# Experts' first matrices split into two float32r parts for the product with the stacked features, and bulk transfers moved in the SyncE queue

## The chip, the cores and the metric

One Trainium2 chip; the program runs on one of its cores. The metric is the device time in microseconds (us) of one execution, and the kernel before and the changed kernel are each run several times. Engines are named as in the profile: PE (TensorE matmuls), PEld (its weight loads), DVE (VectorE), ACT (ScalarE), POOL (GpSimd), SP (SyncE, which only issues transfers). An engine name with q behind it is that engine's instruction queue.

## The reference

The input is `x`, 8 sequences of 512 tokens of 512 numbers. Two layers are applied, each with a condition stage and a feed-forward stage.

```python
# layer 0, condition: a low-rank map chosen by the sequence's language, plus an embedding
t = einsum('bsd,brd->bsr', x, lora_A[lang]); x = einsum('bsr,bdr->bsd', t, lora_B[lang]) + embed[lang]
# layer 0, feed-forward: mixture of 8 experts, 2 for each token, capacity 512 tokens for each expert
weights = softmax(top2(x @ expert_embeddings.T)); index, vals = first 512 tokens of each expert
inter = relu(einsum('ech,eih->eci', tokens, first_linear))      # 512 -> 1024
out = einsum('eci,ehi->ech', inter, second_linear) * vals       # 1024 -> 512, added back by index
# layer 1, condition: additive attention pooling with a mask
# layer 1, feed-forward: two linear layers (512 -> 2048 -> 512), activations in int8,
# weights w1, w2 rounded to -1, 0, 1 with scale 1/mean(|w|)
```

Because the tokens that enter the experts are themselves a product of 100 stacked features (rank rows and language rows) with a matrix of 512 columns, the kernel multiplies that matrix with each expert's first matrix beforehand, and the tokens' 100 features with the result. Float32 accuracy is wanted throughout layer 0.

## The kernel before

The program has three blocks, one behind the other; a barrier stands between them.

**First block (0 to 74 us).** `x_t` is loaded in eight parts, multiplied with the projection, the tokens are routed to experts, and slots are found. The first matrices of experts 0 to 2 (2 MB each, `w_in_sb`, a ring of `AHEAD` = 3) are loaded and multiplied with `lora_b_sb` (`g_product`, L176 to L180): for each half `n` of the 1024 columns, four quarters `k` of the 512 rows, one float32 matmul of 100 x 512 each, accumulated in one PSUM bank.

**Second block (74 to 350 us), the experts.** For each expert `e` (0 to 7) there are eight steps `k` (`KI` = 8), each for 128 of the 1024 inner columns:

- PE: `inner_block` (L907 to L913) makes 128 x 512 inner values in a PSUM bank from `g_0`, `g_1` and the gathered features `rows_0`, `rows_1` with two float32r matmuls; `out_block` (L914 to L927) of the step before makes the outputs with 12 float32r matmuls; `expand` (L931 to L939) makes quarters of the product `lora_b_sb` x first matrix for the expert two further on, at steps 1, 2, 3 (first half) and 5, 6, 7 (second half) of experts 1 to 5 by the table `G_AT`: 8 products for each expert, 40 in all. At step 3 `turn` transposes the features of the next expert.
- ACT: `w_h` (L802, the rounded part of the second matrix), `inner_h` (L806), then by step `take_y`, `high_g`, `take_rows`, and the preparation of layer 1's weights: `sum_abs` (L777, 16 instructions for the mean of absolute values) and `quantise` (L789 and L793, 32 pairs).
- DVE: `w_l` (L868, what rounding left over), `inner_l` (L871), then by step `take_y` (L859), `low_g` (L850, L852), `weights`, `take_rows`. In expert 3 it sums the absolute values at step 0 (L887), PE multiplies that sum with ones at step 1 (L950) ahead of its `out_block`, and DVE makes scales of it at step 2.
- POOL: for each expert it gathers features for the expert two further on (`gather`, L185, four indirect transfers), its slots' choices (L719, four), and adds the outputs of the expert to DRAM (L739, four). The first of these additions waits until all eight parts of `x` have been copied to DRAM (`x1_init`).
- SP issues in the order written in its part (L679 to L713): copies of `x` to `x_after_experts` (1 MB each, `copy_x`), second matrices `w_raw` (1 MB halves, each waits for `w_l_cp`, that is, for DVE to have finished with the buffer), first matrices `w_in_sb` (2 MB), and layer 1's weights `raw` (1 MB groups, two buffers).

```python
def out_block(e, k):
    pe.wait_ge(in_l, KI * e + k + 1)
    pe.wait_ge(w_l_cp, KI * e + k + 1)
...
act.wait_ge(in_mm, i + 1)
if i >= 2:
    act.wait_ge(k_mm, i - 1)
act.activation(inner_h[:, k % 2, :], ps[:, 4 + k % 2, :], ACT.Relu).then_inc(in_h, 1)
```

**Third block (350 to 771 us)** is layer 1. The change doesn't touch its code.

A split into float32r parts, as the kernel uses it for the second matrices: the high part is the value rounded to float32r by a copy, the low part is value minus high part; three products (low x high, high x low, high x high) stand for one float32 product.

## Time and profile before

| | us |
|---|---|
| median of 3 runs | 775.08 |
| lowest and highest run | 775.01 and 776.08 |
| the profiled execution | 772.75 |
| its span (first to last instruction) | 770.8 |
| PE busy | 680.4 (88% of the span) |
| DVE busy | 500.3 (65%) |
| ACT busy | 485.1 (63%) |
| POOL busy | 375.7 (49%) |

The span is what the rows of the trace are measured in, from its start. The profiled execution is 1.95 us longer than its span and 2.33 us shorter than the median of the runs. PE's granted clock is 1.00 where it is at 2.4 GHz, and about half of that where it is at 1.2 GHz. In a timeline row of PE, the starts of consecutive matmuls tell what one costs; its duration is longer, since matmuls overlap. Two matmul instructions of line L179 are one float32 product.

### The profile page before, as it was taken

The numbers are of one execution on the slowest core, as the hardware profiler recorded it, in microseconds if no ns is written. First come the engines' busy times: TensorE is split into PE (matmuls) and PEld (weight loads), VectorE is DVE, ScalarE is ACT, GpSimd is POOL, SyncE is SP. The second block draws the span as 40 slices with busy tenths as digits, with TensorE's granted clock in tenths as the row PEclk, the third lists the DMA queues.
The fourth block names the chain that finished last, engine by engine and source line by source line (L and its number), as shares of the span: only waits on it lengthen the run. The fifth ranks groups of instructions, "written<-read, shape, count | busy, mean of one in ns | idle before, by whom it ended". The sixth has DMA issues, their size and how long they took to land.

```text
span 770.8 us, 9706 instructions
## 1 busy us (share of the span) xinstructions
PE 680.4 (88%) x3152; PEld 416.5 (54%) x3184; DVE 500.3 (65%) x897; ACT 485.1 (63%) x724; POOL 375.7 (49%) x386
## 2 busy tenths in 40 slices
PE   6898689998999999964778889999898998898996
PEld 3333577676777777752455554555455554454442
DVE  3287344544444555524255889888898888999893
ACT  1245236664367778841355878697786977878772
POOL 0202723554342611333575675857758566644463
PEclk9999989999999999985989999999999999999999
DMA  6997949998483937727112021031211110112211
GB/s 214 301 405 284 351 160 369 307 328 295 99 225 146 233 132 162 164 30 239 43 55 83 1 96 55 28 110 51 86 56 42 42 55 29 55 56 69 68 56 68
DMA packets 41699, 108.79 MB, mean 141 GB/s; under 512 B 5393, under 2 KB 6177, under 8 KB 38449
## 3 DMA queue, kind: packets, MB, share of 16 engines
q1 hardware_dynamic: 33712, 94.64, 34.7%
q0 software_dynamic: 7424, 13.06, 9.4%
q10 hardware_dynamic: 512, 0.47, 0.2%
q8 instruction: 25, 0.41, 0.2%
q14 instruction: 26, 0.20, 0.1%
HBM read 88.42 MB, written 28.13 MB: 151 GB/s over the span
## 4 chain that ended last, share of the span: by engine, by line
PE 16%; issue 12%; DVE 11%; POOL 9%; ACT 3%; DVEq 1%; POOLq 0%; ACTq 0%
PE ps L1253 5%; PE ps L1279 5%; POOL ht L1225 3%; POOL xb L1231 2%; DVE h L1686 2%; DVE h_mx L1691 2%; DVE run_max L1652 1%; DVE pool_mx L1608 1%; DVE run_max L1653 1%; PE ps L1303 1%; PE ps L1310 1%; POOL rms L1208 1%; DVEq L1645 1%; POOL qt L1176 1%; PE ps L1312 1%
## 5 line engine op out<-in xcount | busy, mean ns | idle before, releaser
L1253 PE MATMUL ps<-ff_q,qt 128*128 128x512 bf16 x486 | 120.8, 390 | 11.4 <-DVE h L1686 5.1
L1279 PE MATMUL ps<-ff_q,ht 128*128 128x512 bf16 x506 | 121.3, 383 | 4.5 <-DVE res L1699 4.3
L739 POOL DMA_INDIRECT x_after_experts<-y,row_of_slot x32 | 51.2, 1599 | 138.1 <-DVE y L859 109.3
L922 PE MATMUL ps<-w_h,inner_l 128*128 128x512 f32 x256 | 103.7, 405 | 10.0 <-issue 6.6
L924 PE MATMUL ps<-w_h,inner_h 128*128 128x512 f32 x256 | 101.5, 396 | 0.0
L923 PE MATMUL ps<-w_l,inner_h 128*128 128x512 f32 x256 | 101.4, 396 | 0.0
L1686 DVE SCALAR_TENSOR_TENSOR h<-ps,scale,bias 128x1024 f32<-128x1024 f32 x64 | 81.9, 1280 | 24.2 <-PE ps L1253 24.1
L871 DVE SCALAR_TENSOR_TENSOR inner_l<-ps,inner_h 128x512 fp32r<-128x512 f32 x64 | 44.2, 690 | 71.6 <-ACT inner_h L806 53.8
L806 ACT ACTIVATE inner_h<-ps 128x512 fp32r<-128x512 f32 x64 | 38.0, 593 | 82.2 <-PE ps L912 58.5
L1253 PEld LDWEIGHTS ps<-ff_q,qt 128*128 128x128 bf16 x512 | 48.2, 100 | 68.9 <-DVE h L1686 10.2
L1480 ACT ACTIVATE h<-h 128x1024 f32<-128x1024 f32 x64 | 66.7, 1052 | 24.9 <-DVE h L1686 24.7
L1279 PEld LDWEIGHTS ps<-ff_q,ht 128*128 128x128 bf16 x512 | 49.3, 99 | 59.8 <-DVE res L1699 4.6
L1691 DVE TENSOR_REDUCE h_mx<-h 128x1 f32<-128x1024 f32 x64 | 77.4, 1210 | 2.0 <-ACT h L1480 2.0
L868 DVE TENSOR_TENSOR w_l<-w_raw,w_h 128x512 fp32r<-128x512 f32 x64 | 44.2, 690 | 51.3 <-ACT w_h L802 49.2
L1486 ACT ACTIVATE h<-h,to_q 128x2048 int8<-128x2048 f32 x32 | 63.9, 1998 | 13.2 <-DVE to_q L1712 13.2
L1225 POOL TENSOR_SCALAR ht<-hp 128x2048 bf16<-128x2048 int8 x32 | 60.8, 1899 | 5.9 <-DVE hp L1675 5.2
L1554 ACT ACTIVATE h_junk<-h 128x2048 int8<-128x2048 f32 x32 | 61.1, 1911 | 1.0
L922 PEld LDWEIGHTS ps<-w_h,inner_l 128*128 128x128 f32 x256 | 49.0, 192 | 22.4 <-issue 7.0
L179 PE MATMUL ps<-w_in_sb,lora_b_sb 128*100 128x512 f32 x128 | 60.7, 595 | 0.0
L1204 POOL TENSOR_SCALAR mean_sq<-h_sq 128x1 f32<-128x1 f32 x32 | 6.1, 190 | 110.9 <-ACT h_junk L1554 110.8
L924 PEld LDWEIGHTS ps<-w_h,inner_h 128*128 128x128 f32 x256 | 49.0, 191 | 11.5
L923 PEld LDWEIGHTS ps<-w_l,inner_h 128*128 128x128 f32 x256 | 49.2, 192 | 10.4
(251 smaller groups left out, 1330.2 us busy)
## 6 DMA issues: line engine op xcount, KB each, us to landing
w_in_sb<-in_w_in_t SPq DMA_DIRECT2D x8, 2048.0 KB
w_raw<-in_w_out_t SPq DMA_DIRECT2D x16, 1024.0 KB
raw<-in_ff_t SPq DMA_DIRECT2D x16, 1024.0 KB
x_after_experts<-in_x SPq DMA_DIRECT2D x8, 1024.0 KB
x_sum<-x_after_experts SPq DMA_DIRECT2D x8, 1024.0 KB, 4.9
x<-x_after_experts SPq DMA_DIRECT2D x32, 256.0 KB, 2.7
out<-res SPq DMA_DIRECT2D x32, 256.0 KB, 2.3
x_sum<-in_x_t SPq DMA_DIRECT2D x6, 1024.0 KB, 6.6
```

Of the source, the lines that this page charges most:

```text
L179: return pe.matmul(ps[0:STACK_1, bank, :], lora_b_sb[:, k, :], w_in_sb[:, e % AHEAD, k, n * 512:(n + 1) * 512], start=k == 0, stop=k == KD ...
L922: pe.matmul(ps[:, s, :], inner_l[:, k % 2, c], w_h[:, k % RING, :], start=k == 0, stop=False)
L923: pe.matmul(ps[:, s, :], inner_h[:, k % 2, c], w_l[:, k % RING, :], start=False, stop=False)
L924: m = pe.matmul(ps[:, s, :], inner_h[:, k % 2, c], w_h[:, k % RING, :], start=False, stop=k == KI - 1)
L1225: pool.tensor_scalar(ht[:, t % 2, :, :, :], pairs, 1.0, 0.0, ALU.mult, ALU.add).then_inc(ht_ready, 1)
L1253: m = pe.matmul(ps[:, ff_bank(t, half) + n, :], qt[:, t // TPB % 2, t % TPB, k, :], ff1_q[:, k, f * 512:(f + 1) * 512], start=k == 0, stop ...
L1279: mm = pe.matmul(ps[:, out_bank(t), :], ht[:, t % 2, k // 2, k % 2, :], ff2_q[:, k, :], start=k == 0, stop=k == KF - 1)
L1480: act.activation(part, part, ACT.Gelu).then_inc(gelu, 1)
L1486: act.activation(h8[:, t % 2, :], h[:, t % 2, :], ACT.Copy, scale=to_q2[:, t % 2:t % 2 + 1]).then_inc(h8_ready, 1)
L1554: act.activation(h_junk[:], h[:, t0 % 2, :], ACT.Square, accum_out=h_sq[:, t0 % 2:t0 % 2 + 1]).then_inc(h_squared, 1)
L1686: ve.scalar_tensor_tensor(h[:, t % 2, cols], ps[:, bank:bank + 2, :].rearrange("p a c -> p (a c)"), scale1[:, t:t + 1], bias1[:, cols], AL ...
L1691: ve.tensor_reduce(h_mx[:, t % 2, half:half + 1], h[:, t % 2, half * HALF:(half + 1) * HALF], AX.X, ALU.max, apply_absolute_value=True).th ...
```

## The change

1. In the second block each 2 MB first matrix of experts 3 to 7 is no longer multiplied as float32. POOL makes the high part of one quarter (128 x 512) at a time (`split_high`), DVE the low part (`split_low`), each into a ring of `G_RING` = 4; `lora_b_sb` is split once, in expert 0 at step 2 (`u_h` by ACT, `u_l` by DVE). PE makes three float32r products in place of one float32 product. POOL and DVE wait for `part_mm` before a place of the ring is written again.
2. `split_high` stands in POOL's queue: the second half of expert `e + 2` behind the gather of iteration `e`, the first half of expert `e + 3` ahead of its additions.
3. `w_in_sb` becomes a list of separate tensors, three in the first block and two in the second; SP's load of one waits for `win_l_cp`.
4. `raw` and `rounded` use the memory of `x_sum`. SP's queue is rearranged: two copies of `x` and the first two groups of `raw` come later.
5. `sum_abs` runs from expert 1 step 7 to expert 3 step 6 (before: experts 1 and 2), the sum and scale in expert 4 at steps 0 and 1 (before: expert 3, steps 0 and 2), and `quantise` from expert 4 step 2, with two pairs at steps 0 and 1 of expert 7.

```diff
+            w_in_sb = w_in_sb + [sb(a, "w_in_sb2", [P, KD, INNER])]
...
-            QUANT_AT = 4 * KI
+            ABS_AT = 2 * KI - 1
+            QUANT_AT = 4 * KI + 2
+            G_RING = 4
...
+            u_h, u_l = (sb(a, f"u_{i}", [P, KD, STACK_1], F32R) for i in "hl")
+            win_h, win_l = (sb(a, f"win_{i}", [P, G_RING, 512], F32R) for i in "hl")
...
-            raw = sb(a, "raw", [P, 2, GK, D])
+            raw = [x_sum[1], sb(a, "raw", [P, GK, D])]
...
-            rounded = sb(a, "rounded", [P, 2, D])
+            rounded = x_sum[0][:, 0:2, :]
...
+            def quant_steps(e, k):
+                n = e * KI + k - QUANT_AT + max(0, min(k, 2)) * (e == EXPERTS - 1)
+                return range(max(n, 0), n + 1 + (e == EXPERTS - 1 and k < 2))
...
+            part_of = lambda e, n, k: (e - G_FIRST) * 2 * KD + n * KD + k
...
                     sp.wait_ge(rows_in[0], DMA * SB)
-                    for b in (2, 3, 4):
-                        copy_x(sp, b)
+                    copy_x(sp, 2)
...
                             if e + 1 < EXPERTS:
                                 sp.wait_ge(w_l_cp, e * KI + (i + 1) * KI // 2)
                                 sp.dma_start(w_raw[:, i, :, :], w_out_v[e + 1, i]).then_inc(w_raw_in[i], DMA)
                             if e == 0:
-                                load_raw(i)
-                                for b in ((5,), (6, 7))[i]:
+                                for b in ((3, 4), (5, 6, 7))[i]:
                                     copy_x(sp, b)
-                            if e in (1, 2):
-                                load_raw(4 * e - 1 + 2 * i)
+                            if e == 1:
+                                load_raw(i)
...
+                    def split_high(e, n):
+                        for k in range(KD) if G_FIRST <= e < EXPERTS else ():
+                            u = part_of(e, n, k)
+                            if n == 0 and k == 0:
+                                pool.wait_ge(w_in_in[w_in_at(e)], DMA * ((e - G_FIRST) // 2 + 2))
+                            if u >= G_RING:
+                                pool.wait_ge(part_mm, u - G_RING + 1)
+                            pool.tensor_scalar(win_h[:, u % G_RING, :], w_in_sb[w_in_at(e)][:, k, n * 512:(n + 1) * 512],
+                                               1.0, 0.0, ALU.mult, ALU.add).then_inc(win_h_cp, 1)
...
                             gather(pool, e + 2)
+                            split_high(e + 2, 1)
                             pool.wait_ge(w_slot_ready, e + 1)
                             gather_choices(e + 2)
+                        split_high(e + 3, 0)
...
+                    def split_low(e, n, k):
+                        u = part_of(e, n, k)
+                        ve.wait_ge(win_h_cp, u + 1)
+                        if u >= G_RING:
+                            ve.wait_ge(part_mm, u - G_RING + 1)
+                        ve.tensor_tensor(win_l[:, u % G_RING, :], w_in_sb[w_in_at(e)][:, k, n * 512:(n + 1) * 512],
+                                         win_h[:, u % G_RING, :].bitcast(F32), ALU.subtract).then_inc(win_l_cp, 1)
...
+                            if 1 <= e <= EXPERTS - AHEAD:
+                                for n, part in G_AT.get(k + 1, ()):
+                                    split_low(e + 2, n, part)
...
-                            m = g_product(pe, e, n, part, G_BANK)
-                            if part == KD - 1:
-                                m.then_inc(g_mm, 1)
+                            pe.wait_ge(win_l_cp, u + 1)
+                            bank = ps[0:STACK_1, G_BANK, :]
+                            pe.matmul(bank, u_l[:, part, :], win_h[:, u % G_RING, :], start=part == 0, stop=False)
+                            pe.matmul(bank, u_h[:, part, :], win_l[:, u % G_RING, :], start=False, stop=False)
+                            pe.matmul(bank, u_h[:, part, :], win_h[:, u % G_RING, :], start=False, stop=part == KD - 1).then_inc(part_mm, 1)
```

POOL's queue in experts 0 and 1, before (L185 is a gather of features, L719 of choices, L739 the addition of an expert's outputs):

```order
L185 DMA rows<-token_features,row_of_slot 128x100 x4
L719 DMA choices<-token_choices,row_of_slot 128x4 x4
L739 DMA x_after_experts<-y,row_of_slot 4608x512 x4
L185 DMA rows<-token_features,row_of_slot 128x100 x4
L719 DMA choices<-token_choices,row_of_slot 128x4 x4
```

and in the change (line numbers are those of the changed kernel: L736 choices, L769 addition, L748 the high part):

```order
L185 DMA rows<-token_features,row_of_slot 128x100 x4
L736 DMA choices<-token_choices,row_of_slot 128x4 x4
L748 ISA
L748 TENSOR_SCALAR win_h<-w_in_sb 128x512 x4
L769 DMA x_after_experts<-y,row_of_slot 4608x512 x4
L185 DMA rows<-token_features,row_of_slot 128x100 x4
L748 TENSOR_SCALAR win_h<-w_in_sb 128x512 x4
```

The second set of four high parts, which is the second half of expert 3's matrix, stands behind the first additions and a gather.

SP's queue at the start of the second block, before:

```order
L154 DMA x_after_experts<-in_x 128x4x512 [waits rows_in0]
L154 DMA x_after_experts<-in_x 128x4x512 x2
L691 DMA w_in_sb<-in_w_in_t 128x4096
L698 DMA w_raw<-in_w_out_t 128x4x512 [waits w_l_cp]
L686 DMA raw<-in_ff_t 128x2048
L154 DMA x_after_experts<-in_x 128x4x512
L698 DMA w_raw<-in_w_out_t 128x4x512 [waits w_l_cp]
L686 DMA raw<-in_ff_t 128x2048
L154 DMA x_after_experts<-in_x 128x4x512 x2
```

and in the change:

```order
L154 DMA x_after_experts<-in_x 128x4x512 [waits rows_in0]
L707 DMA w_in_sb<-in_w_in_t 128x4096
L715 DMA w_raw<-in_w_out_t 128x4x512 [waits w_l_cp]
L154 DMA x_after_experts<-in_x 128x4x512 x2
L715 DMA w_raw<-in_w_out_t 128x4x512 [waits w_l_cp]
L154 DMA x_after_experts<-in_x 128x4x512 x3
```

Two of the three copies ahead of the first matrix now stand behind the first `w_raw`, and both groups of `raw` are gone from this piece.

DVE's queue in the change, expert 4, steps 0 and 1 (L893 `take_y`, L884 and L886 `low_g`, L900 the low part of a quarter, L934 the sum of absolute values, L910 `w_l`, L913 `inner_l`):

```order
L893 TENSOR_SCALAR y<-ps,w_slot 128x512 x2
L884 TENSOR_TENSOR g<-ps,g 64x512
L886 TENSOR_TENSOR g<-ps,g 4x512
L900 TENSOR_TENSOR win_l<-w_in_sb,win_h 128x512 x2
L934 TENSOR_REDUCE abs_sum<-abs_part 128x2
L910 TENSOR_TENSOR w_l<-w_raw,w_h 128x512
L913 SCALAR_TENSOR_TENSOR inner_l<-ps,inner_h 128x512
```

Before, in expert 3, `abs_sum` stood directly behind `low_g`; now two low parts stand between them.

## Rows read from the trace of the kernel before

**Rows 1.** The page, busy us, share of the span and instructions of each engine.

```profile
PE 680.4 (88%) x3152; PEld 416.5 (54%) x3184; DVE 500.3 (65%) x897; ACT 485.1 (63%) x724; POOL 375.7 (49%) x386
```

**Rows 2.** Stretches: span, busy us of PE, PEld, DVE, ACT, POOL, clock, DMA, GB/s.

```profile
88.00:98.00 10.00, 3.89 (x20) 2.88 (x17) 0.98 (x3) 0.88 (x2) 5.99 (x6) 0.95 1.00 380
118.00:150.00 32.00, 31.48 (x126) 22.54 (x125) 14.34 (x24) 19.24 (x37) 14.24 (x12) 1.00 0.95 319
252.00:285.00 33.00, 33.00 (x133) 23.83 (x132) 16.72 (x28) 24.60 (x40) 13.99 (x12) 1.00 0.63 164
```

**Rows 3.** Groups by line and shape: busy us, mean ns, idle before.

```profile
L179 PE MATMUL ps<-w_in_sb,lora_b_sb 128*100 128x512 f32 x128 | 60.7, 595 | 0.0
L868 DVE TENSOR_TENSOR w_l<-w_raw,w_h 128x512 fp32r<-128x512 f32 x64 | 44.2, 690 | 51.3 <-ACT w_h L802 49.2 <-issue 2.0
L1120 POOL TENSOR_SCALAR x_h<-x_sum 128x2048 fp32r<-128x2048 f32 x8 | 15.2, 1905 | 0.3
L1111 POOL TENSOR_SCALAR side_key_r<-side_key 128x64 fp32r<-128x64 f32 x8 | 1.9, 242 | 2.3 <-ACT side_key L1472 2.3
```

**Rows 4.** Timeline of PE, expert 2, two step ends: start, duration, instruction.

```profile
167.20 0.39 PE L924 MATMUL ps<-w_h,inner_h 128*128 128x512 f32 x1
167.42 0.39 PE L911 MATMUL ps<-rows,g 128*128 128x512 f32 x1
167.65 0.39 PE L912 MATMUL ps<-rows,g 100*128 100x512 f32 x1
...
170.42 0.39 PE L924 MATMUL ps<-w_h,inner_h 128*128 128x512 f32 x1
170.65 1.88 PE L179 MATMUL ps<-w_in_sb,lora_b_sb 128*100 128x512 f32 x4
...
172.59 0.39 PE L912 MATMUL ps<-rows,g 100*128 100x512 f32 x1
```

**Rows 5.** Timeline of expert 0, steps 3 and 4: ACT and PE.

```profile
97.12 0.60 ACT L806 ACTIVATE inner_h<-ps 128x512 fp32r<-128x512 f32 x1 [10.00 <-remote]
...
98.50 0.79 PE L922 MATMUL ps<-w_h,inner_l 128*128 128x512 f32 x1 [6.61 <-issue]
...
103.78 0.44 PE L911 MATMUL ps<-rows,g 128*128 128x512 f32 x1
```

**Rows 6.** Timelines of SP, POOL and PE, end of expert 0 to middle of expert 1.

```profile
111.06 0.38 SPq L698 DMA_DIRECT2D w_raw<-in_w_out_t  x1
...
125.72 1.64 POOL L739 DMA_INDIRECT x_after_experts<-y,row_of_slot  x1 [21.52 <-DMA x_after_experts<-in_x]
...
136.64 1.88 PE L179 MATMUL ps<-w_in_sb,lora_b_sb 128*100 128x512 f32 x4
137.37 0.94 POOL L185 DMA_INDIRECT rows<-token_features,row_of_slot  x1 [0.30 <-issue]
```

**Rows 7.** Timelines of DVE and PE, expert 4, steps 0 and 1.

```profile
222.68 0.70 DVE L852 TENSOR_TENSOR g<-ps,g 4x512 fp32r<-4x512 f32 x1
...
223.43 1.96 PE L179 MATMUL ps<-w_in_sb,lora_b_sb 128*100 128x512 f32 x4
...
224.68 0.69 DVE L871 SCALAR_TENSOR_TENSOR inner_l<-ps,inner_h 128x512 fp32r<-128x512 f32 x1
...
225.69 0.40 PE L922 MATMUL ps<-w_h,inner_l 128*128 128x512 f32 x1
```

**Rows 8.** Timeline, expert 3, step 1: PE waits for the sum.

```profile
187.23 0.38 PE L950 MATMUL ps<-abs_sum,ones 128*128 128x2 f32 x2 [2.91 <-DVE abs_sum L887]
```

**Rows 9.** Timelines of ACT and PE, expert 7, steps 0 and 1.

```profile
315.27 0.80 ACT L789 ACTIVATE rounded<-raw,magic,step_size 128x512 f32<-128x512 f32 x1
316.11 0.72 ACT L793 ACTIVATE ff_q<-rounded,magic 128x512 bf16<-128x512 f32 x1
316.73 0.61 ACT L802 ACTIVATE w_h<-w_raw 128x512 fp32r<-128x512 f32 x1
...
318.73 0.50 PE L922 MATMUL ps<-w_h,inner_l 128*128 128x512 f32 x1 [0.41 <-DVE inner_l L871]
```

More of the change, by code:

```diff
@@ L788, in quantise @@
                             act.wait_ge(quant, u - 1)
-                        act.activation(rounded[:, u % 2, :], raw[:, g % 2, k, :], ACT.Identity, bias=magic[:, 0:1],
+                        act.activation(rounded[:, u % 2, :], raw[g % 2][:, k, :], ACT.Identity, bias=magic[:, 0:1],
                                        scale=step_size[:, i:i + 1]).then_inc(rounded_ready, 1)
@@ L810, in _ @@
                                 high_g(AHEAD - 1, 1)
+                                act.activation(u_h[:], lora_b_sb[:], ACT.Copy).then_inc(u_h_cp, 1)
                             if k == 0 and 2 <= e <= EXPERTS - AHEAD + 1:
@@ L818, in _ @@
                                 sum_abs(abs_step(e, k))
-                            if inside(quant_step(e, k), GK * GROUPS):
-                                quantise(quant_step(e, k))
+                            for u in quant_steps(e, k):
+                                quantise(u)
                     take_y(EXPERTS - 1)
@@ L947, in _ @@
                             inner_block(e, k)
-                            if k == 1 and e == 3:
+                            if k == 1 and e == 4:
                                 pe.wait_ge(abs_ready, 1)
```

54 lines of the change are left out of this document (32 added, 22 removed).

## The prediction

> **What bounds the kernel now.** I read the page first: PE is busy 88% of the span, the other engines 65% or less [rows 1]. Then the busy time by stretches. In the experts' block PE has no idle time in a full expert such as the one from 252 us (33.00 us of 33.00), while POOL has 14 us of work there, DVE 17, ACT 25 [rows 2]. So here time is PE's, and work taken from PE is time gained as long as DVE, ACT and POOL deliver. Third, the timeline, for the places where PE does not run. There are two large ones. In expert 0, ACT stands still for 10.00 us, PE for 6.61 us behind it, and then PE makes its next 12 matmuls from 98.50 to 103.78, 5.28 us [rows 5], at the lower of its two clocks; at full clock 12 cost 2.74 us (below). In this stretch the transfers are at 1.00 of what they can do and move 380 GB/s, the most of all stretches [rows 2]. In expert 3, PE waits 2.91 us for the sum of absolute values [rows 8]. The third block is untouched, and I leave its 420 us as they are.
>
> **The products on PE.** Between the last matmul of an `out_block` and the second of the next `inner_block` lie 0.45 us without products (167.20 to 167.65) and 2.17 us with two (170.42 to 172.59) [rows 4]: 0.86 us for one float32 product. A float32r matmul of the same 512 columns costs 0.23 us (167.42 to 167.65) [rows 4], so three cost 0.69. Forty products: 40 x (0.86 - 0.69) = **-6.8 us**. The product's own group shows its two instructions at 595 ns each [rows 3]; that is latency, and the spacing is what counts. That three replace two instructions needs 40 more weight loads, which lie under the matmuls.
>
> **The low parts on DVE.** 40 instructions of the form of `w_l`, 0.69 us [rows 3]: 28 us, in experts with some 16 us of DVE's time free each [rows 2]. Hidden, but for one place. In step 0 of an expert DVE also has two `take_y` and two `low_g`, and ends these at 223.38 (222.68 + 0.70), when PE is about to start its products at 223.43 [rows 7]. Two low parts end at 224.76, `w_l` and `inner_l` of step 1 behind them at 226.14; PE wanted that `inner_l` at 225.69 less the 0.34 that two cheaper products save, 225.35. PE loses 0.8, say 0.9 with the signals, in experts 2, 3 and 5: **+2.7 us**. In expert 1 there is no `low_g` in step 0, and expert 4 has a larger wait:
>
> **The sum of absolute values.** PE's wait for it, 2.91 us [rows 8], moves from expert 3 to 4, but DVE has two low parts ahead of the sum now: 2 x 0.69 = **+1.4 us**. It takes the place of expert 4's 0.9.
>
> **Layer 1's weights.** Expert 7 gets two more `quantise` pairs on ACT, in steps 0 and 1. One pair costs 315.27 to 316.73 = 1.46 us, and PE already waited 0.41 us for ACT's and DVE's chain there [rows 9]. The first pair is paid in full (1.46); for the second, ACT has some 0.8 us to spare (PE's step is 3.2 us, ACT's is 1.46 and two instructions that add 0.5 each), which leaves 0.6: **+2.0 us**. From step 2 on ACT's step is shorter than PE's again.
>
> **The high parts on POOL.** POOL has this form at 1905 ns for 2048 columns and 242 ns for 64 [rows 3]; on the line between them 512 columns cost 0.62 us, 25 us for 40. POOL has the time [rows 2] but not the place. The second four for expert 3 stand behind the first additions, and these wait for all copies of `x`. Now: SP starts the last 4 MB ahead of the last copy (second `w_raw`, a group of `raw`, two copies) at 111.06; the additions start at 125.72, 14.66 us later; the last gather ends at 138.31, 27.25 us later; PE starts the products of step 5 at 136.64, 25.6 us later [rows 6]. In the change the 4 MB are `w_raw` and three copies, so POOL's times stand. The first high part is there at 27.9, its low part at 28.7. PE is there at 24.9 (four cheaper products earlier in the expert). It loses 3.8, with signals **+4.2 us**. In experts 2 to 5 the additions wait for outputs only, which come about 3 us into the expert; additions and gathers take 12.6 us (125.72 to 138.31), one high and one low part 1.3: 17 us into the expert. PE has six steps of 14 x 0.23 = 3.2 us and four products of 0.69 ahead of these products: 22 us. POOL is early there, less what DVE has queued, by 3 us or so. If that stop of PE brings the lower clock, it costs up to the 2.5 us that it cost in expert 0 [rows 5], after a longer stop; the 2.91 us wait brought none. I take 0, and keep 2.5 for the range.
>
> **SP's queue.** The first matrix is issued before two copies that it stood behind, and the 3 MB at the start (one copy, one first matrix) take 8 us at the rate of that stretch [rows 2] and are done before it begins. This uncovers the stop in expert 0. What ACT waits for there is a signal of PE whose matmuls the timeline shows as done 7 us earlier; the profile names no releaser ("remote"). It falls into the stretch with the heaviest transfers [rows 2, 5]. Nothing there shows how the signal is held up, so the bounds are 0 and all of it: PE's 6.61 us and 5.28 - 2.74 = 2.5 us of slow clock, **-9.2 us**. I take the whole, since the nearest row with the cause away, any later step of the same form, has no such stop. But the stretch from 118 us is at 0.95 too and has none [rows 2]: that speaks against transfers as the only cause. `raw` groups come later and are wanted about 12 us after their issue, 1 MB behind up to 3 MB: 0, at most 2 us. The split of `lora_b_sb` (one ACT and one DVE instruction) lies in expert 0 under PE's `out_block`: 0. `raw` in the memory of `x_sum` costs nothing, since those loads wait for the last additions anyway. Where the cover goes in expert 0, each costs at most 0.69.
>
> **Sum.** -6.8 + 2.7 + 1.4 + 2.0 + 4.2 = +3.5 for the edits to the products and to the order of ACT's, DVE's and POOL's work, and -9.2 for the stop: -5.7 us. From the profiled execution, 772.75, that makes 767.0. The runs' median lies 2.33 us above that execution, so 775.08 - 5.7 = **769.4 us**.
>
> **Rivals.**
>
> *The stop stays (slower).* PE's signal is late for a reason other than the copies; then +3.5 alone: 778.6. For it: the loaded stretch from 118 us without a stop, and that the profile names no releaser. It decides from the point where 3.5 of the 9.2 us or less is gained.
>
> *POOL and DVE hold each other up.* The new low part on DVE and `w_l` read two tensors of SBUF, the high part on POOL reads one. If these two could not run at once, in expert 1 the alternating high and low parts would take two more high parts' time before step 5's second product (1.2 us), and in the tight step 0 to 1 of experts 2 to 5 one (0.62): 4 x 0.62 = 2.5; together +3.7, 773.1. No row here has the two kinds at once. In the Trainium skill, "SBUF — State Buffer", section "Who interferes with whom", a VectorE instruction with two SBUF inputs and a GpSimd instruction that reads SBUF exclude each other for their whole length; by that rule this rival would be what happens, and longer single durations of the two would show it. It is not seen in the trace of before, where POOL in this block only issues transfers. I leave it at a low chance, since most collisions would fall into time that DVE has.
>
> *POOL is late in every expert.* If high parts cost more behind transfers than the two rows say, or gathers are slower, experts 2 to 5 get the wait of expert 1 too: 4 x 4.2 = 16.8, 786.2. Against it: the margin of 3 us.
>
> *Three products cost as much as one.* If the short weight loads of 100 columns do not hide, the 6.8 us do not come: 776.2. Against it: the second matmul of `inner_block` and its load run at 0.23 [rows 4].
>
> **Chances.** What a measurement of this kernel can tell from no change is about 0.2%, 1.6 us. The forecast 0.46; the stop stays 0.30; POOL against DVE 0.11; products not cheaper 0.08; POOL late everywhere 0.05. Faster: the forecast and the collisions, 0.57. Within 0.2%: 0.08. Slower: 0.35. The range: the forecast's terms may be off by 2.5 us of clock and 2 us of `raw` upward, and 3 us downward if POOL's wait is shorter; it reaches to the stop that stays, 778.6, with 2 us for the clock: 766.0 to 780.5. The forecast's own range is 766.0 to 774.0.
>
> **What would show it.** In the profile after: products at 0.23 us spacing, three for each quarter; no 10 us wait of ACT at 87 to 97 us, PEclk at 9 in that slice; a PE wait of about 4 us for the low part in expert 1, released through DVE by POOL; a PE wait of 4 to 5 us for the sum in expert 4; 2 us of waits in expert 7. The forecast is wrong if the stop in expert 0 is there again, at the same place or beside another 4 MB of copies, or if PE waits for low parts in experts 2 to 5 by more than 1 us each.

## The result, and the profile after

| | kernel before | changed kernel |
|---|---|---|
| median of 4 runs each, on one chip | 775.58 us | 787.44 us |
| lowest and highest run | 775.01 and 776.24 | 785.83 and 788.06 |
| the profiled execution, its span | 772.75, 770.8 | 788.06, 786.3 |
| mean granted clock over the span | 0.962 | 0.954 |

The change makes the kernel slower: 1.0141 times the time before (95% interval 1.0103 to 1.0179), where 769.4 us was forecast; it lies above the range, which ended at 780.5. The products came as forecast. Two other steps went wrong: the cause of the stop in expert 0, and the price of the high parts that stand late in POOL's queue.

The page of the changed kernel, busy time and the clock by slices (the first line answers to [rows 1]):

```profile
PE 681.8 (87%) x3224; PEld 429.1 (55%) x3224; DVE 528.6 (67%) x938; ACT 486.0 (62%) x725; POOL 405.2 (52%) x426
...
PEclk9999779799999999997799999999999999999998
```

DVE has 28 us more and POOL 30. PE has 1.4 us more, although its products are cheaper: it runs more of its matmuls at half clock. PEclk, of which each digit is 19.66 us, shows where in the experts' block: at 7 in slices 5 and 6 (79 to 118 us) and in slice 8 (138 to 157).

Where does the time go? In the timelines of PE of both kernels I took the start of each expert's first matmul of `inner_block` (L911 before, L958 after; for the end, that of expert 7's last). The differences of these times are what each expert takes:

| us | start | e0 | e1 | e2 | e3 | e4 | e5 | e6 | e7 | rest |
|---|---|---|---|---|---|---|---|---|---|---|
| before | 77.83 | 35.64 | 32.61 | 34.01 | 36.39 | 33.22 | 33.23 | 28.33 | 23.21 | 436.33 |
| after | 79.11 | 39.63 | 41.28 | 32.65 | 32.66 | 38.89 | 32.63 | 27.82 | 26.11 | 435.52 |
| difference | +1.28 | +3.99 | +8.67 | -1.36 | -3.73 | +5.67 | -0.60 | -0.51 | +2.90 | -0.81 |

They add up to 15.5 us, the difference of the two spans. Expert 0, which was to become 9.2 us shorter, is 4.0 us longer. Expert 1 is the largest single entry. Experts 3 and 4 belong together, since the wait for the sum moves from one to the other.

**Expert 0.** The timelines of ACT and PE, changed kernel (start, duration, instruction, idle time before it and what ended it):

```profile
95.34 0.60 ACT L839 ACTIVATE inner_h<-ps 128x512 fp32r<-128x512 f32 x1 [5.88 <-remote]
105.30 0.60 ACT L839 ACTIVATE inner_h<-ps 128x512 fp32r<-128x512 f32 x1 [8.85 <-remote]
...
96.71 0.79 PE L969 MATMUL ps<-w_h,inner_l 128*128 128x512 f32 x1 [2.94 <-issue]
...
102.42 0.44 PE L959 MATMUL ps<-rows,g 100*128 100x512 f32 x1
106.67 0.80 PE L969 MATMUL ps<-w_h,inner_l 128*128 128x512 f32 x1 [3.81 <-DVE inner_l L913]
```

Where the kernel before stops once for 6.61 us [rows 5], this one stops twice, for 2.94 and 3.81, and both times goes on at the lower clock. Its transfers are not at their limit here: of 88 to 98 us, where the kernel before had a share of 1.00 and 380 GB/s [rows 2], the changed kernel's row reads:

```profile
88.00:98.00 10.00, 7.06 (x31) 5.51 (x30) 4.63 (x10) 2.58 (x6) 7.44 (x9) 0.88 0.55 193
```

So the transfers were spread as meant over the stretch as a whole (0.55, 193 GB/s), and the stop stayed. Within it the load is uneven: from 94.0 to 96.7 us, in the first stop, the share is 1.05. The second stop has almost none beside it (0.02):

```profile
102.90:106.60 3.70, 0.00 (x0) 0.00 (x0) 0.67 (x2) 1.30 (x3) 2.03 (x4) 0.91 0.02 1
```

POOL's timeline shows what else there is. The gathers for expert 2's choices, which came after a gap of 3.37 us in the kernel before, here follow the others with hardly a break, and four high parts behind them:

```profile
96.03 0.95 POOL L185 DMA_INDIRECT rows<-token_features,row_of_slot  x1 [0.30 <-issue]
97.40 1.28 POOL L736 DMA_INDIRECT choices<-token_choices,row_of_slot  x1 [0.42 <-issue]
...
101.48 0.95 POOL L736 DMA_INDIRECT choices<-token_choices,row_of_slot  x1 [0.30 <-issue]
102.55 2.38 POOL L748 TENSOR_SCALAR win_h<-w_in_sb 128x512 fp32r<-128x512 f32 x4
```

**Expert 1.** SP's, POOL's, DVE's and PE's timelines around step 5 (they answer to [rows 6]):

```profile
116.35 0.39 SPq L715 DMA_DIRECT2D w_raw<-in_w_out_t  x1
116.78 2.01 SPq L154 DMA_DIRECT2D x_after_experts<-in_x  x3
...
133.36 1.76 POOL L769 DMA_INDIRECT x_after_experts<-y,row_of_slot  x1 [28.43 <-DMA x_after_experts<-in_x]
...
144.90 0.95 POOL L185 DMA_INDIRECT rows<-token_features,row_of_slot  x1 [0.30 <-issue]
145.88 2.81 POOL L748 TENSOR_SCALAR win_h<-w_in_sb 128x512 fp32r<-128x512 f32 x4
...
146.54 2.69 DVE L900 TENSOR_TENSOR win_l<-w_in_sb,win_h 128x512 fp32r<-128x512 f32 x2 [8.12 <-POOL win_h L748]
...
148.37 0.72 PE L985 MATMUL ps<-win_h,u_l 128*100 128x512 f32 x1 [7.04 <-DVE win_l L900]
```

PE is where it was expected: it ends its work before the products at 148.37 - 7.04 = 141.33, 25.0 us after SP's issue (forecast 24.9). POOL and DVE are late. The additions start 17.0 us after the issue, not 14.66, and end with the gathers 12.5 us later, as before; the four high parts start at 145.88. DVE's first two low parts take 2.69 us together, where two of 0.69 were expected (POOL's high parts run at the same time), and PE starts on the first of them 1.8 us after DVE began it. The wait is 7.04 us where 4.2 was forecast, and PE's clock is low behind it. The stretches with the lower clock in the changed kernel (columns as in [rows 2]):

```profile
95.67:102.50 6.83, 5.79 (x14) 4.46 (x14) 1.78 (x5) 0.78 (x2) 5.12 (x6) 0.50 0.92 349
105.91:112.73 6.82, 6.05 (x14) 4.84 (x15) 2.49 (x4) 1.51 (x3) 0.00 (x0) 0.50 0.01 2
143.46:153.69 10.23, 5.32 (x13) 3.96 (x14) 6.13 (x8) 1.57 (x3) 8.63 (x10) 0.50 0.30 64
232.20:239.03 6.83, 5.77 (x15) 4.56 (x16) 3.79 (x10) 0.00 (x0) 5.61 (x5) 0.50 1.04 235
```

A clock of 0.50 is the level of 1.2 GHz. Some 14 matmuls in each take 0.43 us and not 0.23, about 2.7 us a stretch.

**Experts 4 and 7.** DVE and PE in expert 4, ACT and PE in expert 7:

```profile
230.41 0.68 DVE L884 TENSOR_TENSOR g<-ps,g 64x512 fp32r<-64x512 f32 x1 [1.60 <-ACT g L791]
...
231.84 1.29 DVE L900 TENSOR_TENSOR win_l<-w_in_sb,win_h 128x512 fp32r<-128x512 f32 x2
...
233.26 0.59 PE L998 MATMUL ps<-abs_sum,ones 128*128 128x2 f32 x2 [4.11 <-DVE abs_sum L934]
...
330.95 0.72 ACT L826 ACTIVATE ff_q<-x_sum,magic 128x512 bf16<-128x512 f32 x1
...
333.57 0.50 PE L969 MATMUL ps<-w_h,inner_l 128*128 128x512 f32 x1 [1.90 <-DVE inner_l L913]
```

The wait for the sum is 4.11 us where it was 2.91 [rows 8]: 1.2 more (forecast 1.4), but this time the lower clock comes with it. DVE stands still for 1.60 us in front of `low_g` (L884), behind which its two low parts stand; that will be used below. Expert 7's wait is 1.90 us, 0.41 before [rows 9].

**The parts themselves.** Groups by line and shape, changed kernel, from 79 to 340 us; the first two are the new instructions, the third answers to [rows 3]:

```profile
L900 DVE TENSOR_TENSOR win_l<-w_in_sb,win_h 128x512 fp32r<-128x512 f32 x40 | 28.4, 731 | 8.4 <-POOL win_h L748 8.1
L748 POOL TENSOR_SCALAR win_h<-w_in_sb 128x512 fp32r<-128x512 f32 x40 | 27.0, 692 | 32.7 <-PE ps L987 32.4
L910 DVE TENSOR_TENSOR w_l<-w_raw,w_h 128x512 fp32r<-128x512 f32 x60 | 42.5, 708 | 28.3 <-ACT w_h L835 27.9
```

### The profile page after: what moved, and what is told of

It is laid out like the page before. It is cut to its first block, busy times and chain, and to the rows that moved or that the text cites. A ratio compares the mean times of both kernels' runs of the same rounds, so it can differ in the third digit from the quotient of the medians.

```text
span 786.3 us, 9945 instructions
## 1 busy us (share of the span) xinstructions
PE 681.8 (87%) x3224; PEld 429.1 (55%) x3224; DVE 528.6 (67%) x938; ACT 486.0 (62%) x725; POOL 405.2 (52%) x426
## 4 chain that ended last, share of the span: by engine, by line
issue 14%; DVE 13%; PE 11%; POOL 9%; ACT 5%; DVEq 1%; POOLq 0%; ACTq 0%
PE ps L1327 3%; POOL ht L1273 3%; PE ps L1301 3%; DVE h L1734 3%; DVE h_mx L1739 2%; POOL xb L1279 2%; DVE run_max L1700 1%; ACT h L1528 1%; DVE run_max L1701 1%; DVE pool_sb L1650 1%; PE ps L1358 1%; DVE big L1671 1%; POOL rms L1256 1%; DVEq L1693 1%; PE ps L1351 1%
## 5 line engine op out<-in xcount | busy, mean ns | idle before, releaser
L969 PE MATMUL ps<-w_h,inner_l 128*128 128x512 f32 x256 | 106.3, 415 | 10.7 <-DVE inner_l L913 7.8
L970 PE MATMUL ps<-w_l,inner_h 128*128 128x512 f32 x256 | 104.4, 408 | 0.0
L971 PE MATMUL ps<-w_h,inner_h 128*128 128x512 f32 x256 | 104.2, 407 | 0.0
L769 POOL DMA_INDIRECT x_after_experts<-y,row_of_slot x32 | 52.0, 1624 | 97.3 <-DVE y L893 61.5
L913 DVE SCALAR_TENSOR_TENSOR inner_l<-ps,inner_h 128x512 fp32r<-128x512 f32 x64 | 44.2, 690 | 69.6 <-ACT inner_h L839 62.5
L910 DVE TENSOR_TENSOR w_l<-w_raw,w_h 128x512 fp32r<-128x512 f32 x64 | 45.3, 707 | 33.1 <-ACT w_h L835 32.7
L969 PEld LDWEIGHTS ps<-w_h,inner_l 128*128 128x128 f32 x256 | 50.9, 199 | 24.5 <-DVE inner_l L913 10.5
L971 PEld LDWEIGHTS ps<-w_h,inner_h 128*128 128x128 f32 x256 | 50.8, 199 | 11.5
L970 PEld LDWEIGHTS ps<-w_l,inner_h 128*128 128x128 f32 x256 | 50.9, 199 | 10.8
L1478 ACT ACTIVATE pool_junk<-pool_sb 128x512 int8<-128x512 f32 x32 | 20.0, 625 | 43.7 <-DVE pool_sb L1650 43.3
```

The costliest lines, as they stand in the source:

```text
L769: pool.indirect_dma_start(x1_dram, bass.IndirectOffsetOnAxis(row_of_slot[:, e * SB + s:e * SB + s + 1], 0), y[:, s, :], None, compute_op=A ...
L969: pe.matmul(ps[:, s, :], inner_l[:, k % 2, c], w_h[:, k % RING, :], start=k == 0, stop=False)
L970: pe.matmul(ps[:, s, :], inner_h[:, k % 2, c], w_l[:, k % RING, :], start=False, stop=False)
L971: m = pe.matmul(ps[:, s, :], inner_h[:, k % 2, c], w_h[:, k % RING, :], start=False, stop=k == KI - 1)
```

## The experiments

The kernels were run in three series (the first four below without the pause, the pause with the three that build up the best version, and the last three), each on one chip, with the kernel before run among them. Where medians of two series are compared, the ratios to before say how far that holds. Two theories of the stop in expert 0 stood against each other first: transfers (the forecast's), or POOL's row of indirect transfers, which ends just before PE's signals arrive.

**The order of work without the products.** The kernel before, with the change's order on SP and its steps for the sums and `quantise`; the products stay as they were.

```diff
-                    for b in (2, 3, 4):
-                        copy_x(sp, b)
+                    copy_x(sp, 2)
-            quant_step = lambda e, k: e * KI + k - QUANT_AT
+            def quant_steps(e, k):
+                ...
```

> The kernel before with the change's order in SP's queue, the moved sum_abs, sum and quantise, and no split: first matrices are multiplied as float32, as before. Theory A (the split, by POOL's late high parts in expert 1 and the low clock behind each stop of PE, makes the change slow): 777 to 779 us, that is, 775.6 + 2.0 for expert 7, with expert 1 back at 33 us. Rival B (the moved transfers make it slow): 783 us or more, and expert 0 as long as in the change, 39.6 us.

Measured: 778.76 us, before 775.46; ratio 1.0047 (1.0027 to 1.0068). In the profiled execution, at 782.95 us the slowest of the five, PE stops twice in expert 0, for 1.74 and 8.65 us. The third row is the stretch of the second stop from 100 us on (columns as in [rows 2]):

```profile
93.70 0.50 PE L926 MATMUL ps<-w_h,inner_l 128*128 128x512 f32 x1 [1.74 <-issue]
105.82 0.80 PE L926 MATMUL ps<-w_h,inner_l 128*128 128x512 f32 x1 [8.65 <-DVE inner_l L875]
100.00:105.80 5.80, 0.00 (x0) 0.00 (x0) 0.72 (x2) 1.35 (x3) 0.88 (x1) 0.54 0.03 1
```

The copies are moved here, and the longer stop is 2 us longer than before. From 100 us on it has next to no transfers beside it (0.03, 1 GB/s), and it lasts. The order of the work alone costs 3.3 us, so the parts cost 8.7 more (7.3 by the ratios), in spite of cheaper products. The time is that of theory A, but expert 0 takes 39.44 us, as long as rival B had said (39.63 in the changed kernel), so a long expert 0 comes without the parts too. Expert 4 takes 39.51 us: the wait for the sum is 2.91 us there, as it was in expert 3 before, but is followed by some 7 us at a clock of 0.50.

**The copies alone.**

```diff
-                    for b in (2, 3, 4):
-                        copy_x(sp, b)
+                    copy_x(sp, 2)
...
-                                for b in ((5,), (6, 7))[i]:
+                                for b in ((3, 4), (5, 6, 7))[i]:
```

> The kernel before with the copies of x alone moved in SP's queue (one at the start, two, three). Theory T (transfers hold up PE's signal in expert 0): the stop of ACT at 87 to 97 us goes, 766 to 768 us. Rival P (something on POOL's side holds it up): stop stays, 775 to 777 us.

Measured: 779.76 us; ratio 1.0064 (1.002 to 1.0107).

```profile
100.19 0.80 PE L921 MATMUL ps<-w_h,inner_l 128*128 128x512 f32 x1 [6.66 <-DVE inner_l L870]
```

6.66 us where the kernel before has 6.61, and expert 0 takes 35.50 us (35.64). The move gave nothing there. By itself this doesn't rule transfers out, since with this order they fill the stop again (share 1.03 from 93.5 to 100.2 us); the stops without transfers, above, do that. The 4.3 us that the run costs, which neither theory had, lie behind expert 0: experts 1 to 3 take 7.7 us more than before in the profiled execution. There ACT waits for a group of `raw` that comes late, and PE stops for 2.69 us behind it:

```profile
148.58 1.06 ACT L776 ACTIVATE rounded<-raw 128x1024 int8<-128x1024 f32 x1 [5.95 <-DMA raw<-in_ff_t]
```

**High parts ahead of the additions.** The changed kernel, with the second four high parts of expert 3 moved in POOL's queue from behind expert 0's additions and expert 1's row gathers to ahead of them.

```diff
                             gather(pool, e + 2)
-                            split_high(e + 2, 1)
+                            if e != 1:
+                                split_high(e + 2, 1)
...
                         split_high(e + 3, 0)
+                        if e == 0:
+                            split_high(G_FIRST, 1)
```

> The changed kernel with the four high parts of expert 3's second half ahead of the first additions in POOL's queue. Theory A: PE's wait of 7.0 us in expert 1 for the low part goes, and the low clock behind it: 9 us less, 778 to 779 us. Rival: the additions come later now by what POOL waits for PE's products, and hold up expert 1's outputs: no gain, 785 us or more.

Measured: 775.56 us, 11.9 less than the changed kernel's 787.44 (10.0 by the ratios); ratio to before 1.0012 (0.9989 to 1.0035). Expert 1 takes 31.5 us (41.28 in the changed kernel) and has no wait. POOL's order up to the additions of expert 0 is the changed kernel's, but in this execution its row of gathers had its gap (5.20 us) before the last four, and PE one stop of 7.83 us; expert 0 takes 36.61 us, 3.0 less than in the changed kernel. So whether the gap closes can differ with the same order.

**The choices later.** The kernel before, with the gathers of choices for experts 1 and 2 at the end of expert 0 and not in POOL's first row.

```diff
                     gather_choices(0)
-                    gather_choices(1)
...
-                            pool.wait_ge(w_slot_ready, e + 1)
-                            gather_choices(e + 2)
+                            if e > 0:
+                                pool.wait_ge(w_slot_ready, e + 1)
+                                gather_choices(e + 2)
+                            else:
+                                pool.wait_ge(w_h_cp, KI - 1)
+                                gather_choices(1)
+                                pool.wait_ge(w_slot_ready, e + 1)
+                                gather_choices(2)
```

> The kernel before with the gathers of choices for experts 1 and 2 at the end of expert 0 instead of its start. Rival P (POOL's unbroken row of indirect gathers holds up PE's signals in expert 0): ACT's stop ends when POOL's shorter row ends, about 5 us earlier, 769 to 771 us. Theory T: nothing changes, 775 to 777 us.

Measured: 769.37 us; ratio 0.9933 (0.991 to 0.9957), the first gain. POOL and PE:

```profile
90.09 0.95 POOL L185 DMA_INDIRECT rows<-token_features,row_of_slot  x1 [0.30 <-issue]
99.69 1.35 POOL L719 DMA_INDIRECT choices<-token_choices,row_of_slot  x1 [8.64 <-ACT w_h L807]
...
94.78 0.50 PE L927 MATMUL ps<-w_h,inner_l 128*128 128x512 f32 x1 [1.97 <-DVE inner_l L876]
```

The row ends 4.8 us earlier (95.82 to 91.04), and PE's stop is 4.64 us shorter. The transfers' order is that of before, and they are at a share of 0.95 from 88.0 to 94.8 us, so the shorter stop is not owed to them. PE also goes on at full clock here: expert 0 takes 29.02 us, 6.6 less than before.

**A pause in the row.** This tells a row that is long from a row that ends late. The kernel before, with 12 short instructions on a scratch tile between the gathers of choices for expert 0 and those for expert 1:

```diff
+                    pool.memset(junk[:], 0.0).then_inc(junk_done, 1)
+                    pool.wait_ge(junk_done, 1)
                     gather(pool, 1)
...
                     gather_choices(0)
+                    for n in range(12):
+                        pool.tensor_scalar(junk[:], junk[:], 1.0, 0.0, ALU.mult, ALU.add).then_inc(junk_done, 1)
+                        pool.wait_ge(junk_done, n + 2)
                     gather_choices(1)
```

> The kernel before, with 12 short POOL instructions on a scratch tile (some 4 us together, none of it needed) between the gathers of expert 0's choices and those of expert 1's. Theory A, the signals of PE are held up while POOL issues indirect transfers without a break: in the pause they get through, so PE's stop at 100 us becomes two shorter ones or one that is no longer in spite of POOL's row ending 4 us later; 773 to 777. Theory B, the signals come through when the last of that row of transfers is issued, whatever stands between: the stop is 4 us longer, 779 to 782.

Measured: 770.43 us, before 777.02 in these runs; ratio 0.9923 (0.9896 to 0.9951). Work was added and the kernel became faster by more than expected. POOL, PE, and ACT, whose starts show when PE's signals come:

```profile
84.41 0.94 POOL L721 DMA_INDIRECT choices<-token_choices,row_of_slot  x1 [0.30 <-issue]
85.48 4.82 POOL L731 TENSOR_SCALAR junk<-junk 128x128 f32<-128x128 f32 x12
90.57 0.97 POOL L721 DMA_INDIRECT choices<-token_choices,row_of_slot  x1 [0.27 <-POOL junk L731]
...
104.70 0.94 POOL L721 DMA_INDIRECT choices<-token_choices,row_of_slot  x1 [0.30 <-issue]
...
95.43 0.50 PE L929 MATMUL ps<-w_h,inner_l 128*128 128x512 f32 x1 [0.47 <-issue]
108.59 0.79 PE L929 MATMUL ps<-w_h,inner_l 128*128 128x512 f32 x1 [3.22 <-DVE inner_l L878]
...
88.11 0.60 ACT L813 ACTIVATE inner_h<-ps 128x512 fp32r<-128x512 f32 x1 [1.13 <-PE ps L919]
94.99 0.60 ACT L813 ACTIVATE inner_h<-ps 128x512 fp32r<-128x512 f32 x1 [2.10 <-PE ps L919]
107.22 0.60 ACT L813 ACTIVATE inner_h<-ps 128x512 fp32r<-128x512 f32 x1 [5.91 <-remote]
```

The signal that came 8.9 us late in the kernel before is the one at 88.11: it falls into the pause and comes 0.04 us after the end of its matmul. Two stops of 0.47 and 3.22 us take the place of 6.61. In the profiled executions expert 0 becomes 8.5 us shorter and expert 1, into which the second stop now falls, 6.1 us longer, since the lower clock follows it; that is 2.4 of the 2.8 us by which the spans differ (770.8 and 768.0). The medians say 6.6. Put together, in order of the last row's end (a row: indirect transfers of POOL with no gap over 1 us between; PE's restart is the row with the stop's idle time):

| kernel | transfers in the row | row ends | PE goes on | PE idle |
|---|---|---|---|---|
| choices later | 12 | 91.04 | 94.78 | 1.97 |
| before | 16 | 95.82 | 98.50 | 6.61 |
| copies alone | 16 | 96.23 | 100.19 | 6.66 |
| high parts early | 16 | 96.51 | 101.03 | 7.83 |
| order without products | 20 | 100.87 | 105.82 | 8.65 |
| changed kernel | 20 | 102.43 | 96.71 and 106.67 | 2.94 and 3.81 |
| pause | 12 | 105.64 | 108.59 | 3.22 |

In each kernel PE goes on 2.7 to 5.0 us after the row's end, wherever that is. The idle time grows with the row: 2.0 to 3.2 us behind 12 transfers, 6.6 to 7.8 behind 16, 8.65 behind 20. With 20 in the row, one signal came in the middle of it, at 95.34 in the changed kernel and at 92.32 in the order without products (that is its first stop of 1.74 us). The six kernels below fit in: 12 transfers in the row, PE goes on 2.8 to 4.0 us after its end, idle 0.82 to 1.78.

Signal by signal, the traces of all thirteen kernels say where in a row it begins. Take the time from the end of the matmul that ACT waits for to ACT's start. Where that matmul ended up to 11.0 us into the row (eight or nine gathers), ACT started within 0.05 us, when it was free. The first matmul that ended later than that, 11.6 to 14.2 us into the row, was answered 3.1 to 10.1 us late. The rows of eight gathers at 100 to 112 us delayed nothing. In the later rows of expert outputs, four additions and then eight gathers, the first late signals come 17.5 us or more into the row and are late by 0.7 to 1.9 us only.

**Both moves in POOL's queue.** The changed kernel with the edits of "high parts early" and "choices later".

> The changed kernel with two reorderings of POOL's queue together: the second four high parts of expert 3 ahead of expert 0's additions (775.56 alone), and the gathers of the choices for experts 1 and 2 at the end of expert 0's row of gathers, not in it (769.37 on the kernel before, 6.1 us less). Theory: the stop in expert 0 comes from POOL's unbroken row of indirect transfers, and the late high parts are a second, separate loss, so the two gains add: 775.6 - 6 = 769 to 771, the stop of PE at 94 to 101 us is under 3 us, expert 1 stays at 32 us. Rival: the later gathers hold up PE's signals at their new place, or push the high parts of expert 3 behind it again: then a PE wait of some microseconds at 110 to 120 us or in expert 1, and 773 or more.

Measured: 765.76 us; ratio 0.9862 (0.9815 to 0.9909). Lower than the 769 to 771 of the theory. PE's stop in expert 0 is 1.62 us, and it has no wait in expert 1. The two losses are separate. Together the moves gain 21.7 us on the changed kernel, where the two alone gave 11.9 and 6.1 (by the ratios 21.6, against 10.0 and 5.2); what the difference is has not been tested. Expert 0 takes 29.08 us, 7.5 less than with early high parts alone.

**DVE's order.** On top of it:

```diff
+                            if k == 0 and 1 <= e <= EXPERTS - AHEAD:
+                                split_low(e + 2, 0, 0)
+                                split_low(e + 2, 0, 1)
                             if k == 0 and 2 <= e <= EXPERTS - AHEAD + 1:
                                 low_g(e + 1, 1)
...
-                            if 1 <= e <= EXPERTS - AHEAD:
+                            if k > 0 and 1 <= e <= EXPERTS - AHEAD:
...
-                            if e == 4 and k == 0:
+                            if e == 3 and k == KI - 1:
                                 ve.wait_ge(abs_done, 2 * GROUPS)
```

> The run before this one, and on DVE the two low parts of step 0 ahead of low_g, where DVE waits for ACT, and the sum over the partial absolute values at the end of expert 3 (it stood behind two low parts in step 0 of expert 4). Theory: the PE waits of 0.8 us in experts 2, 3 and 5 and of 4.1 us in expert 4, with its microseconds of lower clock, go: 3 x 0.8 + 4.1 + up to 3 = 6 to 9 us less than the run before this one, 761 to 764. Rival: low_g is then the late one by the same two instructions, and the waits only change their name: no more than the 4.1 us go, 765 to 767.

Measured: 759.54 us; ratio 0.9778 (0.973 to 0.9826), 6.2 less than the run before it and below the 761 to 764 of the theory. The waits of 0.79 us and of 4.11 us are gone; one of 1.05 us for `low_g` is left in expert 2.

**The quantise pairs.** On top of it, the two extra pairs in steps 3 and 5 of expert 7:

```diff
-                n = e * KI + k - QUANT_AT + max(0, min(k, 2)) * (e == EXPERTS - 1)
-                return range(max(n, 0), n + 1 + (e == EXPERTS - 1 and k < 2))
+                n = e * KI + k - QUANT_AT + (e == EXPERTS - 1) * ((k > 3) + (k > 5))
+                return range(max(n, 0), n + 1 + (e == EXPERTS - 1 and k in (3, 5)))
```

> The run before this one, with the two extra quantise pairs of expert 7 in steps 3 and 5 and not in steps 0 and 1. Theory: one extra pair at a time fits into what ACT has to spare after a step or two, so the waits in expert 7 (some 3 us) shrink to 1 us or less: 2 to 3 us less than the run before this one, 758 to 762. Rival: ACT has less than 0.5 us to spare in each step of expert 7 whatever the order, so each pair costs 1 us wherever it stands: no difference over 1 us.

Measured: **757.11 us** (756.55 to 757.61), ratio 0.9748 (0.9702 to 0.9794): 2.5% faster than the kernel before, and the best of all. Expert 7's wait is 0.44 us:

```profile
94.90 0.50 PE L977 MATMUL ps<-w_h,inner_l 128*128 128x512 f32 x1 [1.66 <-DVE inner_l L918]
147.10 0.48 PE L993 MATMUL ps<-win_h,u_l 128*100 128x512 f32 x1 [1.63 <-DVE g L891]
303.31 0.50 PE L977 MATMUL ps<-w_h,inner_l 128*128 128x512 f32 x1 [0.44 <-DVE inner_l L918]
```

From this version three things were taken back one at a time, five rounds each, to weigh them where nothing else hides them (before 775.7 us in these runs).

**The float32 products back.** "The order of work without the products" with the late choices, the early sum and the later pairs.

> The best version so far (757.11) with the products of the first matrices as one float32 product each, as in the kernel before: no high and low parts on POOL and DVE; the order of SP's transfers, the late choices, the sum at the end of expert 3 and the quantise pairs in steps 3 and 5 of expert 7 are kept. It tells what the three products themselves are worth once nobody waits for their parts. Theory: the 0.17 us for each of 40 products that the trace of before gives, 6.8 us, less what PE still waits there (about 1.6 us for low_g in expert 2): 762 to 764. Rival: DVE and POOL in each other's way and the extra clock dips take it back: 757 to 759.

Measured: 763.15 us (761.71 to 766.01); ratio to before 0.983 (0.9797 to 0.9863). The products are worth 6.0 us by the medians, 6.4 by the ratios (0.983 less 0.9748), once nobody waits for their parts. Expert 4 as one stretch, this kernel (33.30 us of PE with 137 matmuls) and then the best version (31.90 with 144):

```profile
206.80:240.10 33.30, 33.30 (x137) 24.30 (x135) 16.93 (x30) 21.87 (x36) 14.78 (x12) 1.00 0.69 205
```

```profile
204.20:236.10 31.90, 31.90 (x144) 25.59 (x143) 21.78 (x38) 21.75 (x36) 19.67 (x20) 1.00 0.71 215
```

1.4 us for eight products is 0.175 each, against 0.17 from the trace of before.

**The high parts late again.**

> The best version so far (757.11) with the second four high parts of expert 3 behind expert 0's additions and expert 1's gathers again, as in the changed kernel. The forecast priced this place at 4.2 us. Theory: the wait is 6 to 7 us, as in the changed kernel, and the lower clock after it adds 2 or more: 8 to 10 us, 765 to 767. Rival: what early high parts saved was mostly the second stop in expert 0, which the late choices remove already: 3 to 5 us, 760 to 762.

Measured: 766.36 us; ratio 0.9872 (0.9838 to 0.9905). That is 9.25 more than the best version, 9.6 by the ratios. This alone costs more than the products gain.

```profile
139.37 0.72 PE L990 MATMUL ps<-win_h,u_l 128*100 128x512 f32 x1 [7.38 <-DVE win_l L902]
```

**The copies' old order.**

> The best version so far (757.11) with the copies of x in the order of the kernel before: three before expert 0, one and two in it. The forecast gave this move 9.2 us, from transfers; the runs put the stop down to POOL's row. Theory: spreading the copies is worth nothing or costs a little (alone it cost 4 us on the kernel before, within its noise): 755 to 758. Rival: with POOL's row short, transfers are what is left of the stop (1.7 us): 759 or more.

Measured: 758.66 us (758.25 to 760.84), ratio 0.9781 (0.9748 to 0.9814): 1.5 more than the best version, 2.6 by the ratios, whose intervals overlap; between the theory's 758 and the rival's 759. The stop in expert 0 is as long as in the best version (1.66):

```profile
95.69 0.50 PE L978 MATMUL ps<-w_h,inner_l 128*128 128x512 f32 x1 [1.56 <-DVE inner_l L919]
```

Where the forecast put 9.2 us of gain, there is between nothing and 2.6, and none of it in the stop.

## Why the prediction was wrong

The forecast was faster, by a term that isn't there; "slower" had a chance of 0.35. Step by step, in the profiled executions, where the sum was -5.7 and +15.5 of span came: 21.2 us to find.

- **SP's queue uncovers the stop (-9.2): failed, 13.2 of the 21.2.** This is the step that decides. It put the stop down to the transfers, since that stretch was the most loaded. But stops go on with next to no transfers beside them (the last 5.8 of 8.65 us in the order without products, all of 3.81 in the changed kernel), and the copies alone leave the stop at 6.66 us. What decides over PE's signals is POOL's unbroken row of indirect transfers, shown by a shorter row (stop 1.97) and by a pause in it (0.47 and 3.22). Of expert 0's +4.0 us, about 3 go with the gap of 3.37 us that closed before the last four gathers (39.63 against 36.61 us with early high parts, where it didn't). That gap is itself a consequence: POOL waits there for `w_slot` of DVE, which is held up with PE's signals, and one signal in the middle of the row closes it. It is not shown that the change closes it. The forecast had read "remote" and "names no releaser" and had a loaded stretch without a stop as evidence against itself, at 0.95 [rows 2]. It also took the signal as 7 us late; the matmul ended at 88.24, and ACT started at 97.12, 8.9 us later. It doesn't speak of POOL's work in that stretch, and POOL was the one engine whose work ended just before the signals came. The rival "the stop stays" had the event right at 0.30, and its 778.6 us lacked the rest of this list.
- **High parts late in expert 1 (+4.2): right in kind and place, too small, 5.8 of the 21.2** (expert 1 changed by +8.67; forecast 4.2 less 1.36 for its products). Three terms: the transfers took 17.0 us and not 14.66; the first low part was there 1.8 us after DVE began it, not 0.7; and the lower clock that was taken at 0 came. Put back by itself into the best version it costs 9.25 us. The rival "POOL is late in every expert" did not come: POOL waits for PE in the others (32.4 of 32.7 us of L748's idle time).
- **Low parts in step 0 to 1 (+2.7): right.** 0.79 us in experts 2, 3 and 5, 2.4 together.
- **The sum (+1.4): size of the wait right, price not.** +1.2 us of wait (4.11 against 2.91), but with it 6.83 us at half clock, 2.7 us of loss. The extra 1.2 us are not shown to bring the clock down: in the order without products the wait at this place was 2.91 us, and the clock fell all the same. Experts 3 and 4 together changed by +1.94 where -0.4 was forecast (+1.4, +0.9 and 16 products): 2.3 of the 21.2.
- **Quantise pairs (+2.0): right within 0.9.** Expert 7 +2.90. Moved apart they gave 2.4 us back.
- **Products (-6.8): right.** 0.175 us each, 6.0 us of time.
- **POOL and DVE hold each other up: a small part.** L748 has a mean of 692 ns, against a median of 0.62 us. Where a two-input instruction of DVE lies beside it, the high part is longer (POOL, then DVE, expert 3's start):

```profile
189.04 1.10 POOL L748 TENSOR_SCALAR win_h<-w_in_sb 128x512 fp32r<-128x512 f32 x1 [3.28 <-PE ps L987]
...
188.97 0.69 DVE L910 TENSOR_TENSOR w_l<-w_raw,w_h 128x512 fp32r<-128x512 f32 x1
```

  DVE ends at 189.66, and the high part has 0.48 us more than the usual. The Trainium skill, "SBUF — State Buffer", section "Who interferes with whom", says that an instruction of VectorE with two SBUF inputs and one of GpSimd that reads SBUF contend for the same read port; the trace agrees (1.10 us against 0.62). Its price, which the rival put at 3.7 us, lies mostly in time that both engines have: on average 0.04 us more for each of 40 low parts and 0.07 for each high part. In expert 1, where the first low part came 1.1 us later than reckoned, it is on the path.

What is left of the 21.2 is +1.28 at the block's start and small amounts of either sign. All seven kernels with the parts start at 78.53 to 79.54 us and the six without at 77.65 to 78.57, so most of that start goes with the parts; by what, no run tells.

What stays open: by what path POOL's row holds up PE's signals. The runs show that and when, not how, and they don't separate POOL's issuing from the traffic of the indirect transfers themselves, since a shorter row and a pause change both. Open too is why a signal came in the middle of a row of 20, and why rows that begin with additions hold signals up less. Whether a direct transfer issued by POOL does the same was not tried.

## What to carry to other kernels

A stop whose releaser the profile names "remote" is read against every engine's timeline, not only against the heaviest load: ask whose work ended just before it did. A row of more than eight gathers on POOL beside a dense PE is worth splitting up, or moving to where PE's waiters have slack: here no signal was late within the first eight. And before work is given to an engine "that has the time", look at the place in its queue: four instructions of 0.62 us behind a wait for bulk transfers cost 9.25 us, more than 40 cheaper products gave, and moving them ahead of it took all of that back.

## What the runs showed of the hardware

- PE's signals are held up late in a row of 12 to 20 indirect transfers of POOL: on time (within 0.05 us) up to 11.0 us into a row of gathers, 3.1 to 10.1 us late from 11.6 us on, in thirteen kernels. Adding 4.82 us of useless work in the middle of the row made the kernel 6.6 us faster. The Trainium skill, "Perfetto Trace Analysis", section "Per-instruction lifecycle: what the profiler-reported window actually captures", says that the spreading of a semaphore's update lies outside the profiled window; the trace agrees (the matmuls show as done, the waiter idle for 5.88 and 8.85 us), but no row shows the delay by itself.
- The lower clock does not follow from the length of a wait alone. PE's wait of 2.91 us for the sum [rows 8] brought none, but the same wait of 2.91 us in the order without products was followed by some 7 us at 0.50, and that of 2.90 us in the copies alone by some 3. In the changed kernel 2.94, 4.11 and 7.04 us brought it. 1.90 us in its expert 7 was followed by a mean clock of 0.62 from 334 to 338.5 us, and 1.74 us in the best version with float32 products by a clock of 0.50 from 94.4 to 97.5, while 1.97 and 1.66 us in two of the faster kernels were followed by matmuls at 0.23 us spacing, the full clock.
